# Normalised rows signalled by two token tiles at a time, and turned into two transit banks claimed together

## The reference, cut to what matters

```python
x = x + tanh(g_xattn[0]) * attention(layernorm(x), ctx)        # softmax over ctx (64 rows) and the own rows (64)
x = x + tanh(g_ffn[0])   * ternary_ffn(layernorm(x))           # silu(x w1) * (x w3), then w2; hidden size 682
x = x + tanh(g_xattn[1]) * wkv(w, u, layernorm(x), ctx)        # recurrence over the 64 tokens of a sequence
x = x + tanh(g_ffn[1])   * moe(layernorm(x))                   # a shared part (256) and 8 experts (128 each), top 2
```

## Time and profile before

| what | before |
|---|---|
| median of 3 runs | 754.02 us (752.9 to 755.68) |
| profiled execution | 754.42 us, its span 752.7 us |
| TensorE busy, mean granted clock | 710.4 us (94%), 0.995 |
| DVE, ACT, POOL busy | 518.3 us, 362.0 us, 331.6 us |
| chain that ended last, by engine | PE 63%, DVE 13%, issue 4%, POOL 4%, ACT 2% |

### The profile page before, as it was taken

One profiled execution on the slowest core, in us unless ns is written; L12 is line 12 of the kernel. 1 busy time (PEld: TensorE's weight loads), 2 busy tenths in 40 slices (PEclk: granted clock), 3 DMA queues, 4 the chain that ended last, 5 costly groups with the idle time before them and its releaser, 6 DMA issues.

```text
span 752.7 us, 13056 instructions
## 1 busy us (share of the span) xinstructions
PE 710.4 (94%) x4612; PEld 592.0 (79%) x4612; DVE 518.3 (69%) x926; ACT 362.0 (48%) x693; POOL 331.6 (44%) x345
## 2 busy tenths in 40 slices
PE   7988978999999999999999999999999999898896
PEld 6776767788878888788877888787877888687786
DVE  4589396775977478774877478874777568799532
ACT  4746625654356535654365535553466444533321
POOL 2005204444538155443537155352637255276364
PEclk9999999999999999999999999999999999999999
DMA  8050000110111011110012011110012010011111
GB/s 290 7 163 33 1 29 1 58 43 29 49 51 58 15 43 57 57 42 14 27 58 83 14 42 56 56 42 14 28 56 79 19 39 30 12 60 43 57 57 56
DMA packets 31875, 37.04 MB, mean 49 GB/s; under 512 B 2958, under 2 KB 23140, under 8 KB 31844
## 3 DMA queue, kind: packets, MB, share of 16 engines
q1 hardware_dynamic: 31844, 36.63, 15.3%
HBM read 32.30 MB, written 4.33 MB: 49 GB/s over the span
## 4 chain that ended last, share of the span: by engine, by line
PE 63%; DVE 13%; issue 4%; POOL 4%; ACT 2%; DVEq 0%; POOLq 0%; ACTq 0%
PE sums L490 16%; PE gate_ps L490 15%; PE up_ps L490 13%; PE transit L490 7%; PE transit L567 3%; PE transit L482 2%; POOL act_sb L1182 2%; POOL hid_l L1173 2%; PE transit L577 2%; PE transit L597 1%; DVE act_sb L1423 1%; DVE act_sb L1421 1%; DVE bn_w L1363 1%; DVE wk L1456 1%; PE transit L621 1%
## 5 line engine op out<-in xcount | busy, mean ns | idle before, releaser
L1173 POOL TENSOR_TENSOR hid_l<-act_sb,hid_h 128x512 fp32r<-128x512 f32 x120 | 164.0, 1367 | 205.3 <-ACT hid_h L971 204.9
L1421 DVE SCALAR_TENSOR_TENSOR act_sb<-act_sb,gate_ps 128x512 f32<-128x512 f32 (+1 forms) x128 | 86.7, 677 | 112.9 <-ACT act_sb L953 112.9
L971 ACT ACTIVATE hid_h<-act_sb 128x512 fp32r<-128x512 f32 (+1 forms) x128 | 80.3, 627 | 116.0 <-POOL act_sb L1182 80.1
L1182 POOL TENSOR_TENSOR act_sb<-act_sb,late 128x512 f32<-128x512 f32 x64 | 97.4, 1523 | 61.5 <-DVE act_sb L1423 59.8
L490 PE MATMUL sums<-down_h,hid_h 128*128 128x256 f32 x320 | 91.9, 287 | 3.9 <-POOL hid_l L1173 3.9
L490 PE MATMUL sums<-down_h,hid_l 128*128 128x256 f32 x320 | 89.9, 281 | 0.0
L490 PE MATMUL sums<-down_l,hid_h 128*128 128x256 f32 x320 | 89.8, 281 | 0.0
L1423 DVE TENSOR_TENSOR act_sb<-act_sb,up_ps 128x512 f32<-128x512 f32 x120 | 82.4, 687 | 4.1
L953 ACT ACTIVATE act_sb<-gate_ps 128x512 f32<-128x512 f32 x80 | 47.2, 590 | 76.6 <-PE up_ps L490 67.5
L490 PEld LDWEIGHTS sums<-down_h,hid_h 128*128 128x128 f32 x320 | 60.3, 188 | 11.0 <-issue 8.3
L490 PE MATMUL gate_ps<-zm_h,gate_h 128*128 128x512 f32 x140 | 60.0, 429 | 9.4 <-DVE act_sb L1423 9.4
(11 more groups left out here) (204 smaller groups left out, 1638.2 us busy)
## 6 DMA issues: line engine op xcount, KB each, us to landing
late<-combine_rows SPq DMA_DIRECT2D x64, 256.0 KB, 3.1
ctx_tok<-in_ctx SPq DMA_DIRECT2D x8, 512.0 KB, 4.1
xa<-in_x SPq DMA_DIRECT2D x7, 512.0 KB, 3.5
out_x<-late SPq DMA_DIRECT2D x7, 512.0 KB, 3.0
wk<-in_L_ffn_w SPq DMA_DIRECT2D x2, 682.0 KB
late<-in_L_ffn_w_down SPq DMA_DIRECT2D x1, 1024.0 KB, 7.6
wk<-in_L_ffn_w_gate SPq DMA_DIRECT2D x2, 512.0 KB, 4.6
wk<-in_L_ffn_w_up SPq DMA_DIRECT2D x2, 512.0 KB, 4.4
```

The costliest lines, as they stand in the source:

```text
L971: nc.scalar.activation(hid_h[0:n, pos], act_sb[0:n, pos], ACT.Copy).then_inc(hid_h_set, 1)
L1173: nc.gpsimd.tensor_tensor(hid_l[:, pos], act_sb[:, pos], hid_h[:, pos].bitcast(F32), ALU.subtract).then_inc(hid_l_set, 1)
L1182: nc.gpsimd.tensor_tensor(act_sb[:, pos], act_sb[:, pos], comb_sb[:, pos], ALU.mult).then_inc(weighted, 1)
L1421: nc.vector.scalar_tensor_tensor(mine, mine, 1.0, gate_ps[pos][0:hidden_rows(chunk)], ALU.add, ALU.mult).then_inc(gated_one, 1)
```

## The change

ACT raises `z_done` after the second and after the fourth token tile, so by two for each block and place. TensorE claims both banks before it turns anything, waits for the first two tiles, turns them for both channel halves, waits for the other two tiles, and turns those. The first bank is full after six transposes in place of four, the second after eight as before. `keys_T` does the same with its fifth matmul behind the second pair. `statistics` counts in fours what it counted in twos and waits for the same moment. No transpose, matmul, copy or DMA is added or taken away.

```diff
             def z_T(t, stage, which, source, n):
-                pe.wait_ge(z_done[stage], t.count(stage, 2, n))
-                for h in range(KH):
-                    turn_rows(t, stage, f"{which}{h}", source, h)
+                banks = [claim(t, stage, f"{which}{h}") for h in range(KH)]
+                for pair in range(2):
+                    pe.wait_ge(z_done[stage], t.count(stage, 4, 2 * n - 1 + pair))
+                    for h, (bank, full) in enumerate(banks):
+                        for r in (2 * pair, 2 * pair + 1):
+                            last = nc.tensor.transpose(bank[:, r * P:(r + 1) * P], source[:, r, h * P:(h + 1) * P], ident[:])
+                        if pair:
+                            last.then_inc(full, 1)
 
             def keys_T(t):
 
-                pe.wait_ge(z_done["W"], t.count("W", 2, 1))
                 if t.fixed and t.i == LAG["W"]:
                     pe.wait_ge(grow_set, 1)
                     pe.wait_ge(pos_set, 1)
-                for h in range(KH):
-                    bank, full = claim(t, "W", f"z2T{h}")
-                    for r in range(NT):
-                        nc.tensor.matmul(bank[:, r * P:(r + 1) * P], zw_row[:, r, h * P:(h + 1) * P], ident[:], start=r == 0, stop=False,
-                                         is_transpose=True, skip_group_check=True)
-                    nc.tensor.matmul(bank[:], grow[:, h * P:(h + 1) * P], minus_pos[:].unsqueeze(1).broadcast_to([2, NS, S]),
-                                     start=False, stop=True, skip_group_check=True).then_inc(full, 1)
+                banks = [claim(t, "W", f"z2T{h}") for h in range(KH)]
+                for pair in range(2):
+                    pe.wait_ge(z_done["W"], t.count("W", 4, 1 + pair))
+                    for h, (bank, full) in enumerate(banks):
+                        for r in (2 * pair, 2 * pair + 1):
+                            nc.tensor.matmul(bank[:, r * P:(r + 1) * P], zw_row[:, r, h * P:(h + 1) * P], ident[:], start=r == 0, stop=False,
+                                             is_transpose=True, skip_group_check=True)
+                        if pair:
+                            nc.tensor.matmul(bank[:], grow[:, h * P:(h + 1) * P], minus_pos[:].unsqueeze(1).broadcast_to([2, NS, S]),
+                                             start=False, stop=True, skip_group_check=True).then_inc(full, 1)
...
             def normalise(t, stage, n, rows_in, rows_out, rstd, shift):
...
                 for r in range(NT):
                     last = nc.scalar.activation(rows_out[:, r], rows_in[:, r], ACT.Identity, bias=shift[:, r:r + 1],
                                                 scale=rstd[:, r:r + 1])
-                last.then_inc(z_done[stage], 1)
+                    if r % 2:
+                        last.then_inc(z_done[stage], 1)
...
             def statistics(t, stage, n, rows_in, bn, mv):
                 if not t.fixed or t.count(stage, 2, n) > 1:
-                    dve.wait_ge(z_done[stage], t.count(stage, 2, n - 1))
+                    dve.wait_ge(z_done[stage], t.count(stage, 4, 2 * n - 2))
```

## The result

The changed kernel takes 757.88 us (median of 22 runs, 755.17 to 761.56), the kernel before, run beside it, 755.73 (22 runs, 752.85 to 758.77). The ratio, with its 95% interval, is 1.0043 [1.003, 1.0056]: slower by about 3.2 us (the two medians are 2.15 apart). The forecast was 754.8, 0.8 us above before, and the range ended at 757.3, 3.3 above before. Both stood on 754.02, the median of 3 runs of the kernel before; the 22 runs beside the change put it at 755.73. So 1.7 of the 3.1 us between the forecast time and the measured one lie in this base and not in the change. The profiled execution took 760.28 us with a span of 758.4; that is 5.7 more than in the profile of before, 1.0 of it at the start, where the first DMA of the context landed later. All ratios leave out one single run, of the experiment e8, which took 1388.35 us.

What follows compares the result with a forecast made beforehand. TensorE's own instructions were taken to bound two thirds of the span, unchanged by the edit. The terms 0.99 - 0.20 - 0.06 + 0.1 = +0.8 us on the median of 754.02 gave 754.8 us, range 752.6 to 757.3.

Steps and rivals of the forecast that it cites:

- The two claims: `keys_T`, turn 1: claiming both banks first starts `context_out` 0.99 us later, without cover; bounds 0 and 1.33.
- The clock: TensorE's clock falling behind the longer idle time ahead of `keys_T` in turn 1: 1.7 us, kept as a rival only.
- the rival: First rival: the clock falls in turn 1 behind 2.09 us of idle, costing 1.7 us; time 756.5, chance 0.13.
- DVE's wait in `statistics`: DVE's wait for `z_done` in `statistics`: it asks for the same moment, so no cost was counted.
- The first banks that come later: Turns 2 to 7: first bank full 0.20 us later, taken as 0.02 a turn, 0.1 in all; bounds 0 and 1.2.
- the second wait on TensorE: One more wait in the middle of the transposes at each of 32 places: 0, upper bound 3.4 us.
- second rival: The wait in the middle breaks the stream of transposes in the full turns: 3.4 us, time 758.2, chance 0.08.
- z1T, -0.20: z1T of turn 1: first pair turned during the wait, so ACT reads the first bank 0.20 us earlier; bounds -0.40 and 0.
- z0T, -0.06: z0T of turn 0: the first bank is full 0.06 us earlier; bounds -0.26 and 0.
- z1T of turn 0 and z3T of turn 8: Pairs give nothing at either place: DVE's rest has no idle time before it; a wait for POOL hides the 0.20.

Runs made afterwards that it cites:

- e8: e5 with 37 in place of 30 products of ones ahead of z1T in turns 0 and 1; 754.38 us, 0.9973 of the kernel before.
- e2: The kernel before with only the two bank claims of `keys_T` put together, nothing in pairs; 758.8 us, 1.0024 of the kernel before.
- e4: The whole change with 14 in place of 6 products of ones behind z1T of turn 0; 759.89 us, 1.0049 of the kernel before.
- e3: The whole change with eight products of ones ahead of `keys_T` in turn 1; 757.28 us, 1.0017 of the kernel before.
- e11: The whole change with products of ones at every idle place found in turns 0, 1 and 8; 755.24 us, 1.0004 of the kernel before.
- e6: The whole change, but `keys_T` claims its second bank just ahead of the first transposes into it; 756.47 us, 1.0016 of the kernel before.
- e12: e10 with a semaphore of its own for the first pair, so `z_done` counts by two again; 754.27 us, 0.9975 of the kernel before.
- e10: Pairs in `z_T`, `keys_T` as before, products of ones at every idle place found; 753.29 us, 0.9977 of the kernel before.
- e9: The kernel before with products of ones at every idle place found in turns 0, 1 and 8; 753.54 us, 0.9971 of the kernel before.
- e1: The changed kernel with `keys_T` alone as before, pairs kept in `z_T`; 754.68 us, 0.9988 of the kernel before.
- e5: e1 with seven products of ones in turn 8 ahead of its third expert chunk; 754.75 us, 0.9984 of the kernel before.
- e7: The kernel before with 40 in place of 30 products of ones ahead of z1T in turns 0 and 1; 753.87 us, 0.9968.

## Why the prediction was wrong, step by step

**The two claims, +0.99 forecast.** The mechanism was right, the size was 1.30, near the upper bound of 1.33. I let the ten matmuls start at 85.01, 0.05 behind the last copy, since the second half did so the earlier trace rows. But there TensorE came from work, while now it waits: it starts at 87.77, 0.25 behind the copy's end (85.12 + 2.40). A wait for the bank alone makes 0.14 of that (83.88 behind a copy that ends at 83.74 before the change, 85.39 behind 85.25 in e2). The other 0.11 is a second waiting instruction: the changed order waits for the rows behind the claims, and the trace has two waits of TensorE behind the copy there (87.56 and 87.67) and one before (83.78). The ten take 89.89 - 87.77 = 2.12 in place of 2.01. That the delay has no cover was right: `row_max` came by the claims and the clock later (3.86 + 1.69 = 5.55).

**The clock, left out of the sum.** This is the step that failed most: the sum put a fall of the clock behind the longer wait at nothing, and it cost 1.69 of about 3.2 us. I gave the rival 0.13, because the trace had one case for it (1.91 us of idle in turn 8) and one against (2.83 us at z1T of turn 1). Its size, 1.7, is met by the 1.69 of this profile, but with luck: in e2 and e4 the same fall costs 3.2 and 3.1. Its chance was not right: of the kernels with the grown wait, all three profiles where it isn't filled show the fall (the change, e2, e4), and where ones fill it neither does (e3, e11). The Trainium skill, "TensorE: Matmul & The Clock Gate", section "HAM oscillation — how this bites in real kernels", describes a kernel in which waits between bursts of matmuls, longer than the 2.29 us here, make the next burst start cold; the prediction took that for a wait of this length too. At `keys_T` the trace shows such a fall behind 2.29 us; at z1T of turn 1 it does not in the change, 1.93 us of idle being followed by a window at 1.00, and it does behind 1.93 us in e3 and e6. And the profile of before held a third case that I didn't use: z1T of turn 0, with the longest wait of all. The window behind it:

```profile
48.15:51.00 2.85, 2.76 (x13) 2.48 (x13) 2.78 (x7) 2.72 (x3) 0.00 (x0) 0.50 0.68 193
```

The clock was at 0.50 there; it cost nothing, because it lay under ones (the FFN starts at 51.01, 0.10 behind DVE's rest, as it does after the change), and so I passed over it. That made two falls in three long waits, and the rival's 756.5 the likelier forecast. What decides between these places is not settled.

**The base.** The 754.8 was built on 754.02, from 3 runs; beside the change the kernel before has 755.73. This 1.7 us belongs to no step of the mechanism.

**DVE's wait in `statistics`, costed at nothing.** The prediction said that it "asks for the same moment". The moment is the same, but the wait shared its value with another, and with that the order on VectorE: 0.08 to 0.12 in each of turns 3 to 7, 0.4 to 0.6 in all. The two counts 2i - 2 stand in the code. The Trainium skill, "Perfetto Trace Analysis", section "Identifying Dependency Chains", says that an instruction with several waits may get instructions ahead of it that carry the further waits; the trace of the kernel before shows that (307.34). In the changed kernel a register instruction carries the further wait, 0.09 ahead of the statistics.

**The first banks that come later, +0.1, and the second wait on TensorE, 0 (second rival, 3.4).** Both are 0 in the full turns: e12 keeps both in `z_T` and its turns take 85.63 us, and for `keys_T` e11 and e10 differ by 0.01. At z3T ACT does read the first bank 0.22 later against z3T (303.46 - 302.61 = 0.85, before 0.63), and the last FFN gate comes later with it, but ACT's instruction behind it doesn't (307.10 - 302.61 = 4.49, before 4.50). That was the prediction's own working.

**z1T, -0.20 and z0T, -0.06.** Right: 0.22 in turn 1, and from the context's transposes to `context_out` of turn 0 15.16 in e10 against 15.22 in e9. z1T of turn 0 and z3T of turn 8 give nothing, as forecast. What the pairs did bring at z1T of turn 0 is not in the prediction. The wait is now in two parts (2.24 and 0.27), the clock stays up under the ones behind it, they end sooner, and TensorE waits 2.05 for DVE's rest; the fall that lay under the ones before (12 records in 2.76 us) then lies on the FFN. TensorE in turn 0, after:

```profile
48.48 1.50 PE L458 MATMUL up_ps<-ones 128*128 128x128 f32 x12
...
52.03 0.47 PE L490 MATMUL gate_ps<-za_h,w 128*128 128x512 f32 x1 [2.05 <-DVE za_l L1383]
```

How often that is so over all executions stays open: the profiles of e1, e5 and e6 show it too, and e1 is not slower than before.

**The sum with what was measured** is 1.30 - 0.22 - 0.06 + 0.55 = 1.57 (0.55 is five turns of 0.11, from the runs with ones; the changed kernel's own profile has 0.40), and e11 less e9 is 1.70. With the fall behind `keys_T` it is 3.26, and the ratio says 3.2 [2.3, 4.2]. That they meet so closely is partly luck: that fall costs 1.7 in one profile and more than 3 in two others, and the falls elsewhere vary from one execution to the next.

## What to carry to other kernels

A claim of two buffers together makes the first user wait for the later of the two: look up when each comes free, and what the longer idle time does to the clock of the work behind it. A semaphore that is counted finer changes the value in every wait on it, so look for waits in a loop that shared their value with another, and give the finer signal a semaphore of its own. To price one part of a change, fill the idle places of both kernels first, and compare turn with turn.

## What the runs showed that was not expected

- TensorE's clock can fall behind 0.96 us of idle (e7) and stay up behind 1.93 (the change, z1T of turn 1), and behind 1.93 at the same place it falls in e3 and e6: the length of the wait does not decide by itself.
- Preventing a fall in one place gained nothing where a longer one followed (e4: `context_out` 6.23 in place of 5.36); the fall behind `keys_T` cost 1.7 us in one profile and more than 3 in two others.
- Two waits on VectorE that no longer share a value: the wait for the residual moves to a register instruction ahead of the statistics, which costs 0.08 to 0.10 us at its place, and the same 0.1 at the end of the turn on TensorE.
- A transpose that waited for its bank alone comes 0.14 us behind the copy that frees it (before, e2), one with a second waiting instruction behind that 0.25 (the change, e3, e11), and one that TensorE reaches from work 0.05.
